# A fused state-space, attention and expert network on one core: a repeated period of 308 steps replaced by one list of 4,848 steps

## What is computed

```python
x = x + ssm(ln(x))        # in_proj, 4-tap causal conv, 32 heads, decay x level weights, gated norm, out_proj
x = x + ffn(ln(x))        # 16-head attention, ln, 8 dense experts weighted by the top 2 gates, ln
x = x + shift_mix(ln(x))  # sum over 9 rolls of v(x), each times its own sigmoid gate, ln
x = x + ffn(ln(x))        # the same weights as the first ffn

# inside ssm, for head h of 32:
att = (C @ B.T) * exp(gc[t] - gc[s]) * lam[t, level(t, s)]     # causal
y = att @ (x * dt) + D * x
out = rmsnorm(y * silu(z)) @ out_proj.T
```

## Time and profile before

| | before |
|---|---|
| median of 3 runs | 2105.55 us (2104.37 to 2105.72) |
| the profiled execution, own time | 2103.15 us |
| its span in the trace | 2101.4 us |
| mean granted TensorE clock | 0.966 |
| busy: PE / DVE / ACT / POOL | 91% / 83% / 71% / 37% |
| instructions in the trace | 48245 |

### The profile page before, as it was taken

How to read it: one execution, slowest core, us unless ns; L and a number is a source line. 1 busy time by engine, 2 the same in 40 slices (tenths; PEclk the granted TensorE clock), 3 DMA queues, 4 the chain that set the end, 5 groups by cost and what they waited for, 6 DMA issues and landing times.

```text
span 2101.4 us, 48245 instructions
## 1 busy us (share of the span) xinstructions
PE 1921.0 (91%) x16928; PEld 1491.0 (71%) x16928; DVE 1738.5 (83%) x4463; ACT 1488.0 (71%) x3207; POOL 775.6 (37%) x1139
## 2 busy tenths in 40 slices
PE   4779899999999999999999999999999999997757
...
PEclk8889999999999999999999999999999999998867
...
DMA packets 224576, 117.14 MB, mean 56 GB/s; under 512 B 124360, under 2 KB 210512, under 8 KB 219216
## 3 DMA queue, kind: packets, MB, share of 16 engines
...
## 4 chain that ended last, share of the span: by engine, by line
PE 64%; DVE 23%; ACT 4%; issue 4%; SPq 2%; POOL 2%; DMA 1%; DVEq 0%; ACTq 0%; POOLq 0%
DVE nmax L1295 6%; PE psA L862 6%; PE psB L724 6%; DVE work L1220 5%; PE psB L874 5%; PE psA L874 5%; PE psA L699 5%; PE psB L803 3%; PE psB L862 3%; PE psA L630 3%; PE psB L699 2%; PE psA L803 2%; DVE att L1247 2%; DVE hid L1408 2%; PE psA L788 2%
## 5 line engine op out<-in xcount | busy, mean ns | idle before, releaser
L1247 DVE TENSOR_TENSOR att<-att,QK 128x1024 f32<-128x1024 f32 x192 | 251.2, 1341 | 15.2 <-ACT att L1003 15.1
L1529 POOL TENSOR_TENSOR own<-X,ccoef 128x512 f32<-128x512 f32 x128 | 160.2, 1257 | 206.7 <-PE psA L699 97.1
L1437 POOL TENSOR_SCALAR var_eps<-lnmv 128x2 f32<-128x2 f32 x128 | 40.4, 316 | 524.0 <-DVE lnmv L1110 521.3
L1220 DVE SCALAR_TENSOR_TENSOR work<-psA,c_conv_w,work 128x255 f32<-128x255 f32 (+2 forms) x450 | 195.4, 474 | 11.8 <-ACT work L961 11.8
L630 PE MATMUL psA<-xnT_a,c_w_in 128*128 128x256 f32 x608 | 177.9, 397 | 17.8 <-DVE hid L1220 8.7
L1072 ACT ACTIVATE hid<-psA,c_b 128x256 f32<-128x256 f32 x295 | 135.8, 485 | 79.4 <-PE psA L862 79.2
L1295 DVE TENSOR_REDUCE nmax<-psB 128x2 f32<-128x512 f32 x288 | 186.6, 680 | 1.1 <-PE psB L765 1.1
L862 PE MATMUL psA<-x1T,c_w 128*128 128x256 f32 x608 | 178.9, 394 | 1.5 <-DVE nmax L1295 1.3
L1049 ACT ACTIVATE pt<-psB 128x512 f32<-128x512 f32 x256 | 147.4, 614 | 31.5 <-PE psB L789 31.4
L1295 DVE TENSOR_REDUCE nmax<-psA 128x2 f32<-128x512 f32 x224 | 149.8, 681 | 15.1 <-PE psA L765 14.9
L1220 DVE SCALAR_TENSOR_TENSOR work<-psB,c_conv_w,work 128x255 f32<-128x255 f32 (+1 forms) x360 | 159.0, 474 | 2.7 <-ACT work L961 2.1
...
## 6 DMA issues: line engine op xcount, KB each, us to landing
...
k_max<-qk_scr SPq DMA_DIRECT2D x128, 64.0 KB, 2.0
q_max<-qk_scr SPq DMA_DIRECT2D x128, 64.0 KB, 2.0
...
```

What stands on the lines that cost most here:

```text
L1220: m = e.scalar_tensor_tensor(out=cv[:, back:], in0=t[:, 0:T - back], scalar=conv_w[:, c, tap:tap + 1], in1=cv[:, back:], op0=ALU.mult, op1 ...
L1247: e.tensor_tensor(att[:, :, :], att[:, :, :], bc(QK[:, kq, :], 1, HG), ALU.mult).then_inc(att_done, 1)
L1529: e.tensor_tensor(own_b[k % 2][:, :].rearrange("p (h c) -> p h c", c=HD), X[:, tt, h0 * HD:(h0 + HG) * HD].rearrange("p (h c) -> p h c", c ...
```

## The change

`PERIOD`, `START` and the turn loop are gone. `ORDER` is one text with a word for every step of every batch, `name.step.batch@banks`, in the order in which the engines walk it; the table loads are still put in by the same rule. The steps are the same 4,848, each once per batch and layer, and so are all instructions of the steps. What may differ is the order at any place, and the banks, which are now given per batch. Five waits are added, all on counters that were there before, because an order that doesn't repeat no longer implies them.

```diff
-PERIOD = """
-up0.2+3@03 relu0.3+3 silu0.1+1 load_x0.0+0 ocopy1.3+4 up0.3+3@51 lvl0.0+1 lvl0.1+1 down0.2+3@7 experts1.3+5
...
+ORDER = """
+load_x0.0.0 gates0.0.0 gates0.1.0@0 gates0.2.0@12 conv0.0.0@34 conv0.5.0@56 conv0.2.0@70 tap0.0.0 load_x0.0.1 gates0.3.0 gates0.4.0@1 cpart0.0.0
...
+smax1.1.15@4603 sload1.0.15 up1.6.14@71 relu1.5.14 relu1.6.14 smax1.2.15@4761 down1.6.14@0 rowmax1.2.15 smax1.3.15@3476 rowmax1.3.15 down1.5.14@1
+maxt1.0.15@3 exps1.0.15 es1.0.15@4761 acc1.5.14 es1.1.15@3047 relu1.7.14 exps1.1.15 ep1.0.15@6 down1.7.14@1 es1.2.15@5230 ep1.1.15@4 acc1.6.14
...
-        name, rest = word.split(".")
-        step, n = rest.split("@")[0].split("+")
-        yield name[:-1], int(name[-1]), int(step), int(n)
...
+        name, step, rest = word.split(".")
+        n, _, used = rest.partition("@")
+        yield (name[:-1], int(name[-1]), int(n), int(step)), tuple(int(b) for b in used)
...
 def order():
...
+    for hop, _ in hop_words(ORDER):
+        what, _, n, step = hop
         needed = ("silu_set" if what in SILU_SET else "exp_set" if step in EXP_SET.get(what, ()) else held)
         if needed != held:
             hops.append((needed, 0, n, 0))
             held = needed
-        hops.append((what, lay, n, step))
+        hops.append(hop)
     return hops
...
+    banks = dict(hop_words(ORDER))
...
-        for j, b in enumerate(banks.get((hop[0], hop[1], hop[3]), ())):
+        for j, b in enumerate(banks.get(hop, ())):
...
+                    e.wait_ge(*empty(("sum", 0, n, NU // 2 * (k + 1) - 1)))
...
+                    if hop == first_up[lay, n]:
+                        e.wait_ge(*empty(("tail", lay, n, 4)))
...
+                        e.wait_ge(*empty(("zgate", 0, n, 2 * hg), 1))
...
+                    if nth[hop]:
+                        e.wait_ge(nmax_ready, nth[hop])
...
+                        e.wait_ge(*empty(("xt", 0, n, 2 * hg)))
```

More of the change, by code:

```diff
@@ L134 @@
[L134 to L148, removed]
@@ new lines @@
+up1.1.0@67 xt0.5.3@0 silu0.8.3 experts1.0.0@2 mix1.11.1@6 xcopy0.5.3 down1.1.0@5 smax0.3.2@7124 wexp0.0.3 weigh0.0.3@63 rowmax0.3.2 relu1.2.0
+down1.0.0@0 up1.2.0@67 wexp0.3.3 relu1.3.0 experts1.1.0@3 weigh0.3.3@16 mix1.12.1 xt0.7.3@2 up1.3.0@74 maxt0.0.2@3 gates0.1.4@1 fn1.0.1 acc1.0.0
+acc1.1.0 wexp0.2.3 xcopy0.7.3 wexp0.1.3 weigh0.2.3@67 coef0.0.3 exps0.0.2 prod0.0.3 weigh0.1.3@43 gates0.2.4@01 down1.2.0@6 es0.0.2@5724 sum0.0.3@3
+acc1.2.0 fn1.1.1@0 prod0.1.3 own0.0.3 prod0.2.3 weigh0.4.3@1657 own0.1.3 wexp0.4.3 own0.2.3 sum0.1.3@2 relu1.4.0 up1.4.0@40 own0.3.3 q1.0.1@1
@@ new lines @@
+down1.1.1@5 rowmax0.3.3 weigh0.0.4@24 xcopy0.7.4 up1.2.1@70 wexp0.3.4 weigh0.3.4@21 sload0.0.3 xt0.7.4@4 mix1.12.2 maxt0.0.3@7 up1.3.1@30
+weigh0.2.4@42 fn1.0.2 gates0.1.5@1 own0.0.4 acc1.0.1 acc1.1.1 wexp0.2.4 weigh0.1.4@67 wexp0.1.4 down1.2.1@5 coef0.0.4 prod0.0.4 relu1.3.1 exps0.0.3
+gates0.2.5@14 es0.0.3@2671 sum0.0.4@3 fn1.1.2@0 own0.1.4 own0.2.4 prod0.1.4 prod0.2.4 own0.3.4 sum0.1.4@4 weigh0.4.4@2761 gated0.0.4 up1.4.1@03
+wexp0.4.4 q1.0.2@2 exps0.1.3 ep0.0.3@4 own0.4.4 own0.5.4 gated0.1.4 es0.1.3@7561 relu1.4.1 ocopy0.0.3 q1.1.2@2 sum0.2.4@7 acc1.2.1 exps0.2.3 ep0.1.3@5
@@ new lines @@
+up1.0.4@23 zact0.7.7 xt0.6.7@1 xcopy0.6.7 zgate0.1.7@72 mix1.10.5@3 experts1.0.4@5 relu1.1.4 rowmax0.2.6 smax0.2.6@6135 up1.1.4@40 experts1.1.4@4
+mix1.11.5@6 xt0.5.7@0 xcopy0.5.7 rowmax0.3.6 smax0.3.6@1365 zact0.1.7 weigh0.0.7@40 xt0.7.7@7 silu0.8.7 wexp0.0.7 down1.1.4@2 down1.0.4@1 wexp0.3.7
+weigh0.3.7@34 up1.2.4@60 relu1.2.4 relu1.3.4 up1.3.4@53 mix1.12.5 maxt0.0.6@4 gates0.1.8@6 wexp0.2.7 fn1.0.5 own0.0.7 acc1.0.4 down1.2.4@0 xcopy0.7.7
+own0.1.7 acc1.1.4 coef0.0.7 weigh0.2.7@15 wexp0.1.7 prod0.0.7 weigh0.1.7@32 exps0.0.6 acc1.2.4 gates0.2.8@46 es0.0.6@1507 sum0.0.7@3 fn1.1.5@4
```

402 lines of the change are left out of this document (373 added, 29 removed).

## The result

| | before | after |
|---|---|---|
| median | 2105.64 us (2104.37 to 2108.69) | 2145.35 us (2141.97 to 2150.46) |
| profiled execution, own time | 2103.15 us | 2150.46 us |
| ratio | | 1.0189 (95%: 1.0167 to 1.0211) |

The changed kernel is 1.9% slower. The forecast of 2087.5 us and its range were wrong, and so was the sign. The profiled execution of after is 5 us above its median.

A forecast was written before the change was run, and what follows sets the result against it. PE was taken as the bound, idle 3.58 us of a 119.35 us steady turn. Steady turns -9.1 (-0.7 x 13), fill -4 and drain -5 made -18.1 us: 2085.05 profiled, 2087.5 us median, range 2068 to 2116.

The forecast's parts named there:

- The bank of `up1.0`, of `mix1.10`, of `sum0.6`: Three PE waits for banks in each steady turn, expected to shrink by 0.6 of 0.77, 0.3 of 0.71, 0.4 of 0.43 us.
- the tanh that I had feared: New PE wait on a tanh, at the bank up1.0 takes second; with it only 0.6 of 0.77 us was booked.
- The drain: Last batch: two down steps moved ahead of the last maxt, into a 3.3 us wait; -5 us, bounds 0 and -10.
- The fill: Start of the run: conv steps moved earlier, to fill a hole and shorten a wait for taps; -4 us, bounds -5.2 and +6.
- The five waits: Added waits on counters long reached in the old order; booked 0, bounded by 0.05 us a turn.
- The table loads: Useless pair for mix1.12 at the heads' start, 2.57 us of ACT a turn, mostly hidden; +0.3 us a turn.
- "Give back 0.3": Steady turns: allowance for new waits in each turn's different list, 0.3 us a turn, cutting the gain from 1.0 to 0.7.
- DVE against POOL, 0: Meetings of att on DVE with own on POOL expected mostly to stay; nothing booked, at most 1.20 us a turn.
- The rival "the table loads decide": Heads' start: all 2.57 us of the load pair reach PE each turn; +11.4 us in all, 2117 us; chance 0.18.

The follow-up runs named there:

- e3: Kernel before, order unchanged, every bank dealt by its time of emptying in the profiled execution, plus the five added waits: 2087.32 us, ratio 0.9920.
- e4: Kernel before for its first 4480 steps, then the changed kernel's list with its banks for the last 448, the drain: 2096.43 us, ratio 0.9961.
- e2: Kernel before, order and banks unchanged, with two more table loads between wexp0.3 and wexp0.2 in 14 turns: 2157.12 us, ratio 1.0248.
- e1: Changed kernel, list and banks unchanged, in which mix1.12 no longer asks for a table (68 loads in place of 96): 2125.86 us, ratio 1.0097.
- e5: Kernel before with e3's banks and e4's drain put together: 2079.22 us, ratio 0.9875.
- e10: Kernel of e3 with the changed kernel's order in the heads alone, in 11 turns, banks dealt anew by measured emptying times: 2100.99 us, ratio 0.9976.
- e11: Kernel of e3 with the changed kernel's order in gate products and mix alone, in 11 turns, banks dealt anew by measured times: 2104.01 us, ratio 0.9986.
- e13: Kernel of e3 with the changed kernel's order in second attention, experts and conv alone, 11 turns, banks dealt anew by measured times: 2098.58 us, ratio 0.9972.
- e16: Kernel of e5, banks dealt by its own times, with place0.0 moved ahead of tap0.7 in 14 turns and banks dealt anew: 2091.54 us, ratio 0.9949.
- e12: Kernel before, with the product own on POOL computed for one head of its eight: 2094.20 us, ratio 0.9939.

## Why the prediction was wrong

- *The bank of `up1.0`, of `mix1.10`, of `sum0.6`*: the mechanism was right, the three waits went; that the total fits is in part luck. e3 won 18.8 us where these terms had 1.3 x 13 = 17, but 0.9 us a steady turn and not 1.3, and 5.5 us in the drain, for which the terms had nothing. A new wait of 0.62 us came on DVE's `work`, not on the tanh that I had feared.
- *The drain*: right in sign, off in size; e4 won 9.6 us for the 5 booked, near the far bound. The place was another: the waits on the last maxima, `nmax_bf`, sum to 6.8 us in e4 for 6.6 before, and it was the waits of the score products on the load of `q_max` (8.2 for 10.5 us) and on `nmax` (2.9 for 7.3) that shrank. *The fill*: `weigh0.0` starts at 65.6 us (forecast 65). The second L1367 is at 200.3 us for 203.1, but the third is at 306.7 for 306.4, so the 4 us did not stay.
- *The five waits*: e3 has them and won what the banks were booked for, and e2, which has them with the order and banks of before, is explained without them (53 us for 51), so nothing speaks against 0; they were not run alone.
- *The table loads*: **a step that failed.** I had the right place, price and number (97 loads were forecast and are there), but took 0.3 of 2.57 us a turn, by ACT's idle time over a turn (26.8 us) and a slack "of a size that no row gives", concluded from PE running on without a wait. The row was there: I had read 1.30 us of idleness in 12 us, and the windows have 1.5 in 20, beside a full PE. In e2 2.2 us a turn reach PE, and the clock, for which I had no term, adds some 1.6. In the changed kernel the same loads cost 19.5 us, 1.4 a turn, where that turn is longer already and the two loads stand apart. That either is the reason is not shown.
- *"Give back 0.3"*: **the step that failed most.** I priced an unknown order at 0.3 us a turn, 4 us in all, though I had compared only the three places where before waited. The new order costs 46.6 us (e1 less e5), and it is spread over all three stages (e10, e11, e13). e16 shows how one moved step can do it: a microsecond on a full queue ahead of something that PE waits for. That the other moves work the same way is not shown, and PE's waits don't show it: most of the loss is longer busy time and a low clock, which a sum of waits like mine can't hold.
- *DVE against POOL, 0*: right for the change ("I therefore expect most meetings to stay": `att` at 1347 ns after 1341), and by e12 the whole effect is 12 us in the list of before.

From 2105.6 us: banks and drain -26.7 (e5, measured at 2079.2), order of fill and steady turns +46.6, useless loads +19.5, which is 2145.3. The rival "the table loads decide" had their 33.4 us at the most and nothing for the order; it was right in sign and would have missed by 28 us. Some 5 to 10 us of the order's loss are not located in a stage, and for the stages other than the mix no single move was tried.

The Trainium skill, "ScalarE: Activation LUTs" (What ACT_TABLE_LOAD costs), gives a load 1283 ns and a drain of about 1380 ns. No run here shows the drain: in e2 a load starts 0.02 us after the copy before it ends and the next follows 1.28 us later. The estimate of the loss from this page's figures (69 us in 13 turns, all on the path) lies nearer to e2's 51 us than my 4, but by another mechanism: there it was waits and clock.
